# Moving the turn of a graph network's sums behind two chunks of the next pair, and the counts of edges behind the low parts

## The reference

```
layer 0:  a = (1 + eps) * x + segment_sum(x[src], dst)
          h = relu(batch_norm(a @ W1 + b1));  h = relu(batch_norm(h @ W2 + b2))   # W1 512x1024, W2 1024x512
          x1 = layernorm(x + (x + h))
layer 1:  a = segment_sum(x1[src], dst);  a = where(in_degree > 0, a, x1)
          h = relu(a @ W.T + b);  h = batch_norm(h)                                # W 512x512
          out = layernorm(x1 + h)
```

## Time and profile before

| | us |
|---|---|
| three runs | 2587.13, 2593.28, 2592.99; median 2592.99 |
| the profiled execution | 2588.04 |
| its span, first to last instruction | 2586.3 |
| busy: PE | 2295.0 (89%) |
| busy: POOL | 1602.0 (62%) |
| busy: DVE | 1364.4 (53%) |
| busy: ACT | 801.0 (31%) |

### The profile page before, as it was taken

How to read it: one execution, slowest core, us unless ns; L and a number is a source line. 1 busy time by engine, 2 the same in 40 slices (tenths; PEclk the granted TensorE clock), 3 DMA queues, 4 the chain that set the end, 5 groups by cost and what they waited for, 6 DMA issues and landing times. The chain is left out here.

```text
span 2586.3 us, 41697 instructions
## 1 busy us (share of the span) xinstructions
PE 2295.0 (89%) x9657; PEld 1505.0 (58%) x9658; DVE 1364.4 (53%) x2155; ACT 801.0 (31%) x1272; POOL 1602.0 (62%) x1729
## 2 busy tenths in 40 slices
PE   4999999999999999799995299999999999999964
PEld 2666666666666666688884255555555555555544
DVE  5555555555555555533336555455545555554557
ACT  1333333333333333455548411111111111111157
POOL 6777777777777777100002467777777777777712
PEclk9999999999999999899996699999999999999976
DMA  8777778787877877433216767777777777777758
GB/s 259 233 227 242 224 236 245 220 249 231 242 242 225 251 222 245 142 112 95 93 49 190 255 193 223 210 225 220 219 224 213 226 222 217 223 225 216 224 138 285
DMA packets 180571, 545.11 MB, mean 211 GB/s; under 512 B 48787, under 2 KB 51178, under 8 KB 175794
## 3 DMA queue, kind: packets, MB, share of 16 engines
q0 software_dynamic: 125120, 410.09, 53.5%
q1 hardware_dynamic: 33880, 78.23, 10.1%
q10 hardware_dynamic: 21544, 56.48, 6.5%
HBM read 493.06 MB, written 51.62 MB: 211 GB/s over the span
## 5 line engine op out<-in xcount | busy, mean ns | idle before, releaser
L780 PE MATMUL psum<-ring,select 128*125 x2600 | 1260.9, 608 | 11.0 <-issue 8.7
L555 POOL DMA_INDIRECT ring<-x_in,staged x782 | 799.1, 1022 | 246.2 <-issue 224.0
L555 POOL DMA_INDIRECT ring<-x_d,staged x782 | 748.2, 957 | 261.4 <-issue 226.4
L780 PEld LDWEIGHTS psum<-ring,select 128*125 128x125 f32 x2600 | 479.3, 191 | 380.3 <-issue 336.0
L651 DVE TENSOR_TENSOR rows_lo<-ring,rows_hi 128x512 fp32r<-128x512 f32 x500 | 329.8, 689 | 283.8 <-ACT rows_hi L867 283.2
L867 ACT ACTIVATE rows_hi<-ring 128x512 fp32r x500 | 295.0, 625 | 479.3 <-SPq L523 335.9
L808 PE MATMUL psum<-sumsT_hi,w_hi 128*128 128x250 f32 x1248 | 400.6, 321 | 4.3 <-DVE sumsT_lo L674 4.3
L765 PE MATMUL psum<-rows_hi,select_r 128*125 128x512 f32 x500 | 376.0, 752 | 7.5 <-DVE rows_lo L651 4.2
L808 PE MATMUL psum<-sumsT_lo,w_hi 128*128 128x250 f32 x1248 | 350.1, 281 | 0.0
L808 PE MATMUL psum<-sumsT_hi,w_lo 128*128 128x250 f32 x1248 | 348.4, 279 | 0.0
L808 PEld LDWEIGHTS psum<-sumsT_hi,w_hi 128*128 128x128 f32 x1248 | 237.3, 190 | 36.1 <-issue 32.6
(11 more groups left out here) (168 smaller groups left out, 2255.2 us busy)
## 6 DMA issues: line engine op xcount, KB each, us to landing
hidden_d<-of_layer ACTq DMA_DIRECT2D x25, 1000.0 KB, 5.4
act_f<-hidden_d SPq DMA_DIRECT2D x24, 1000.0 KB
ring<-x_in,staged POOLq DMA_INDIRECT x782, 3.8
ring<-x_d,staged POOLq DMA_INDIRECT x782, 3.7
own<-x_in ACTq DMA_DIRECT2D x50, 224.0 KB
own<-x_d ACTq DMA_DIRECT2D x50, 224.0 KB
ring<-x_d SPq DMA_DIRECT2D x10, 1120.0 KB
x_d<-done_r SPq DMA_DIRECT2D x9, 1120.0 KB
```

The lines of the kernel that those rows point to most:

```text
L555: nc.gpsimd.indirect_dma_start(slot(s), None, table, bass.IndirectOffsetOnAxis(ap=staged[:, s:s + 1], axis=0)).then_inc(gathered[s], 16)
L780: whole = nc.tensor.matmul(agg(h), select[h][:, WHOLE_AT.index(p), :], of_chunk(pe, first, place), start=False, stop=n + 1 == WINDOW, skip ...
```

## The change

The turn of the pair before is now called inside the first scatter of a pair, behind its first two chunks; only bank 0 is cleared ahead of them, and bank 1 inside `turn`, behind its wait for the sums. The address of that clear is taken from a register, which is 1 in a pair's first group and 2 later, so that it then hits a bank that the transposes write anyway. In layer 1 the two counting reductions are taken out of `selection` and called on their own: tile 0's behind `low_part`, tile 1's ahead of the next pair's selection.

```diff
--- before.py
+++ after.py
@@ -636,14 +636,14 @@
                     nc.vector.tensor_tensor(select[h][:, SPLIT:, :], m.column_ps[:, None, :].broadcast_to([P, rest, z.NT]),
                                             local[h][:, 2 * SPLIT:, None].broadcast_to([P, rest, z.NT]), ALU.is_equal
                                             ).then_inc(select_done[h], 1)
-                    if layer == 1:
-                        dve.wait_ge(select_done[h], 2 * v + 2)
-                        with nc.allow_low_precision(reason="counts up to WINDOW are exact in bfloat16"):
-                            nc.vector.tensor_reduce(edge_count[h][:, 0, :],
-                                                    select_r[h][:].bitcast(F32).rearrange("p k n -> p n k"),
-                                                    AX.X, ALU.add)
-                            nc.vector.tensor_reduce(edge_count[h][:, 1, :], select[h][:].rearrange("p k n -> p n k"),
-                                                    AX.X, ALU.add).then_inc(counted[h], 1)
+
+                def counts(v, h):
+                    dve.wait_ge(select_done[h], 2 * v + 2)
+                    with nc.allow_low_precision(reason="counts up to WINDOW are exact in bfloat16"):
+                        nc.vector.tensor_reduce(edge_count[h][:, 0, :],
+                                                select_r[h][:].bitcast(F32).rearrange("p k n -> p n k"), AX.X, ALU.add)
+                        nc.vector.tensor_reduce(edge_count[h][:, 1, :], select[h][:].rearrange("p k n -> p n k"),
+                                                AX.X, ALU.add).then_inc(counted[h], 1)
 
                 def low_rows(v, h, first, a, b):
                     for k in range(min(a, SPLIT), min(b, SPLIT)):
@@ -703,12 +703,16 @@
                         read_sums(v, tiles(pair, 1), 1)
                         low_rows(v, 0, first[0], 0, 2)
                         low_part(v)
+                        if layer == 1:
+                            counts(v, 0)
                         low_rows(v, 0, first[0], 2, 5)
                         selection(v, 1, tiles(i, 1), first[1])
                         low_rows(v, 0, first[0], 5, SPLIT)
 
                         read_sums(v, tiles(i, 0), 0)
                         low_rows(v, 1, first[1], 0, 4)
+                        if layer == 1:
+                            counts(v, 1)
                         next_pair = within(dve, (v + 1) // groups, z.PAIRS, "v counts below pairs times groups")
                         selection(v + 1, 0, tiles(next_pair, 0),
                                   first_chunk(dve, tiles(next_pair, 0), dve.snap((v + 1) % groups)))
@@ -746,12 +750,11 @@
                 def agg(h):
                     return m.bank(h)[0:z.NT, :]
 
-                def clear(i, h):
-                    pe.wait_ge(sums_done[h], i * groups + 1)
-                    nc.tensor.matmul(agg(h)[:, 0:1], m.zeros[:, 0:z.NT], m.ones[:, 0:1],
-                                     start=True, stop=False, skip_group_check=True)
-
-                def scatter(i, v, g, tile, h):
+                def clear(out):
+                    nc.tensor.matmul(out, m.zeros[:, 0:z.NT], m.ones[:, 0:1], start=True, stop=False,
+                                     skip_group_check=True)
+
+                def scatter(i, v, g, tile, h, between):
                     tile_use = pe.snap(2 * v + h)
                     first = first_chunk(pe, tile, g)
 
@@ -759,6 +762,8 @@
                     pe.wait_ge(sums_done[h], v + 1)
                     pe.wait_ge(select_done[h], 2 * v + 2)
                     for n, p in enumerate(ORDER):
+                        if n == 2:
+                            between()
                         if p in SPLIT_AT:
                             k = SPLIT_AT.index(p)
                             pe.wait_ge(split_lo, SPLIT * tile_use + k + 1)
@@ -784,10 +789,14 @@
                         if n + 1 in PRODUCT_AT[h]:
                             product(v, PRODUCT_AT[h][n + 1])
 
-                def turn(job):
+                def turn(job, bank=None):
+
                     pe.wait_ge(lo_done, 2 * job + 1)
                     for h in range(2):
                         pe.wait_ge(sums_done[h], job + 1)
+                    if bank is not None:
+                        at = within(pe, bank * m.BANK, 2 * m.BANK, "bank 1 or 2")
+                        clear(m.psum[0:z.NT, bass.ds(at, 1)])
                     for k in range(z.KD):
                         for h in range(2):
                             at = (k % (z.KD // 2)) * z.W + h * z.NT
@@ -819,14 +828,17 @@
                     pe.wait_ge(weights_lo, 1)
                     nc.tensor.matmul(count_ps[0:z.NT, 0:z.TILES], m.zeros[:, 0:z.NT], m.ones[:],
                                      start=True, stop=False, skip_group_check=True).then_inc(counts_zeroed, 1)
+                cleared = pe.alloc_register(f"pe_cleared{layer}")
                 with pe.Fori(0, z.PAIRS) as i:
-                    clear(i, 0)
-                    clear(i, 1)
+                    pe.wait_ge(sums_done[0], i * groups + 1)
+                    clear(agg(0)[:, 0:1])
+                    pe.reg_mov(cleared, 1)
                     with pe.Fori(0, groups) as g:
                         v = of_use(pe, i, groups, g)
-                        turn(v)
-                        scatter(i, v, g, tiles(i, 0), 0)
-                        scatter(i, v, g, tiles(i, 1), 1)
+
+                        scatter(i, v, g, tiles(i, 0), 0, lambda: turn(v, pe.snap(cleared, min_val=1, max_val=2)))
+                        scatter(i, v, g, tiles(i, 1), 1, lambda: None)
+                        pe.reg_mov(cleared, 2)
                 uses = pe.snap(groups * z.PAIRS)
                 turn(uses)
                 for b in range(HALVES):
@@ -1408,6 +1420,7 @@
 
         m.hidden_stored = nc.alloc_semaphore("hidden_stored")
         m.bank = lambda b: psum[:, b, :]
+        m.psum, m.BANK = psum[:].rearrange("p b c -> p (b c)"), 512
         m.banks = lambda a, b: psum[:, a:b, :]
         m.column_ps = psum[:, 6, 0:z.NT]
         m.column, m.ident = sb("column", [P, P]), sb("ident", [P, P])
```

## The result

Five runs of the kernel before and five of the changed one: median 2593.24 us before, 2580.76 us after (2572.14 to 2582.23); the ratio is 0.9945, 95% interval 0.9929 to 0.9962. That is 12.5 us less, where 2572 was predicted. The profiled execution of the changed kernel took 2581.07 us (span 2579.2), so beside the one before (2588.04) it shows only 7.0 us of the 12.5. The changed kernel's runs fall into two groups, 2572 to 2575 and 2581 to 2582, as those before did with 2587 and 2593; why, the traces don't say.

A forecast was written before the change was run, and what follows sets the result against it. PE and POOL were taken to run in step, with POOL's gathers limiting gains. Layer 1's 13.8 us and layer 0's 4.0 made 17.8, so 2570.2 from 2588.04; allowing for two run groups, 2572, range 2563 to 2581 (72%).

The forecast's parts named there:

- The bound: Both gather phases: PE and POOL run in step, and POOL's gather issue, 1.257 us each in layer 1, limits any gain.
- The rival in which PE gains all: Both layers: PE is the bound and its whole saving counts, about 64 us, giving 2524 us; chance 4%.
- The bubble: Each pair's end: PE's idle time between the clears of banks 0 and 1 goes, saving 1.2 us net, bounds 0.8 and 1.3.
- rival 2: Pair ends: the bubble comes back as another wait, only the start of layer 1 gains, 2583 us; chance 10%.
- POOL's gaps: Layer 1: the second gap, 1.26 us of excess, stays and five later ones, 4.7 us, vanish; layer 0's at 93.33 gives 1.0.
- Start of layer 1: First turn of layer 1: PE starts its chunks before the counts, so POOL's 7.92 us wait shrinks by 5.0, bounds 4.2 and 7.6.
- Tail of layer 1: End of layer 1: the last chunks' lead over PE shrinks from 4.3 to about 0.2 us, gaining 4.1, bounds 1 and 4.7.
- Layer 0: Layer 0: 1.0 us from the gap at 93.33 and 3 from a shorter stretch of slow gathers, 4.0 together.
- The step that failed: Layer 1's gathers: POOL's own length stays 0.957 us each; collisions with subtractions were priced in layer 0 only.
- The clock: Layer 1: PE, starved, falls to 1.2 GHz more often; at twice layer 0's share the time is 2624 us; chance 5%.
- The counts: Layer 1's moved reductions keep their cover of 8 us and cost 0; if cover were gone, up to 4.3 us a pair.
- The signs named ahead: Layer 1: POOL's waits on PE below 10 us, start gap about 3, last gather about 14 earlier, landing waits up, second clear unidled.

The follow-up runs named there:

- e0: The changed kernel itself, run again as reference and source of the second trace: median 2585.07 us, 0.9965 of the kernel before; its profiled execution took 2574.95 us.
- e4c: The changed kernel with only one of three terms of layer 1's product kept, leaving out low parts there: 2579.01 us, 0.9945 of the kernel before.
- e3b: The changed kernel with layer 1's subtraction reading its first operand from PSUM, so its low rows are wrong: 2567.23 us, 0.9898 of the kernel before.
- e5: The changed kernel with a second ACT copy of layer 0's split chunks into PSUM bank 7, which DVE subtracts from: 2580.55 us, 0.995 of the kernel before.
- e1: The changed kernel with the counts back in selection, so only the turn moved, on a slower chip: 3048.05 us against 3070.26 for the kernel before, 0.992.

## Why the prediction was right or wrong

**The number.** 17.8 us were added up and 12.5 measured (8.9 in the runs beside e0); 2580.76 us lies just inside the forecast's own range, whose upper end was 2581. By the profiled executions the sum is 17.8 and the measure 7.0, or 13.1 with the second trace. So the kind of gain was right and its size too large, and that the range held is in part luck: two terms for PE were off in opposite ways and cost nothing, and one was matched by chance.

**The bound: right.** POOL's gathers were named as what the time falls back to once PE runs freely. Layer 1's waits for landings and e4c show it. The rival in which PE gains all, 60 us, is out. The prediction called PE "only just the slower" in layer 1; by its own numbers, 39.27 us a pair against 31.28 gathers at 1.257 us, or 39.3, the two were even. That is why so little came of what PE saved.

**The bubble: right in kind, wrong in size, too small in layer 1 and too large in layer 0.** 1.2 us a pair were predicted, bounds 0.8 and 1.3. In layer 1 PE's pair took 36.67 us while it ran freely. Before, a pair at the full clock took 38.88 us (1565.10 to the next clear at 1603.98): 2.2 us are saved. From the clear of bank 0 to the first product it is 7.56 us for 9.74 one pair earlier; about half of that lies between the two clears and in the two chunks, and the rest is shorter pauses of PE behind them, such as the 0.41 us between the second clear and the transposes, now 0.03, which the sum didn't have. In the other seven of the 24 pairs before, the clock fell, and they took 40.6 us; so 39.27 was a mean of two kinds of pair. In layer 0 the bubble mostly came back as another wait. From 85 to 440 us PE's mean pair went from 39.25 to 38.91 us, 0.3 us less. PE's waits from 100 to 400 us, before and after:

```profile
PE psum L751 <- DVE sums L666: 9.4, 7, 1.5
...
PE psum L770 <- DVE rows_lo L651: 10.7, 14, 1.1
```

The first split chunk now stands right behind the transposes, and its low rows are not ready. That was rival 2, in one layer. Neither error cost the forecast much, since what PE saves in a pair is worth nothing where POOL is the bound.

**POOL's gaps.** In layer 1 the second stayed (1.25 us for 1.26) and the other five vanished (4.7 us), as said; so did the one at 93.33 us in layer 0 (1.0 us).

**Start of layer 1: right in kind, too large.** 5.0 us were predicted, 3.5 measured (7.62 to 4.10 of excess; 4.3 in the second trace). PE started its two chunks 8.1 us sooner on the clock, of which 2.0 are the earlier start of the layer, but they took 3.77 us for 2.91 before and the second clear comes behind them.

**Tail of layer 1: too large.** 4.1 us predicted, 2.6 measured. The prediction took the lead at the end of the last tile but one to shrink from 4.3 to 0.2 us. Its last chunk was issued at 2440.67 and taken at 2445.97: 1.6 us. PE had been stopped for landings earlier in that tile (1.56 us at 2433.36 and 0.79 at 2435.27), and the product behind them let the lead grow again.

**Layer 0: 4.0 predicted, 3.3 measured, but that they agree is chance.** The reason given for 3 of the 4 us, a shorter stretch of slow gathers, isn't seen: the mean gather is the same 1011 ns from 500 to 1000 us, and the time over 0.946 us a gather went from 59.8 to 57.9 us in all. The first gap, for which nothing was predicted, went from 4.14 to 2.88 us of excess, and it is 2.89, 4.14 and 5.40 in three other traces with the same layer 0 (e0, e3b, e4c); the gap at 55 us grew from 0.89 to 1.91. The spread of those four traces, 7.5 us at the last gather, is larger than the gain.

**The step that failed: the gathers of layer 1 keep their length.** The sum took 0.957 us as POOL's own in layer 1 and priced the collision of subtractions and gathers in layer 0 only. It grew in layer 1: the time over 0.946 us a gather went from 9.2 to 15.1 us (14.8, 17.6 and 17.2 in e0, e4c and e5), and with it 6.3 us of the 8.3 us that the waits gave back. e3b shows the cause, the subtraction with two SBUF inputs. Why the same number of meetings now costs more is open: that PE, ACT and DVE follow the landings, and so meet POOL's 1.25 us rhythm in a fixed phase, fits the rows but was only argued. The Trainium skill (SBUF — State Buffer, "SBUF: two separate sides") has the exclusion; the prediction named it and looked for it in the wrong layer. Of the 10.8 us between 17.8 and 7.0 this step is 6.3, start and tail 3.0 together, and the stretch between the layers 1.3, which is no more than traces of one code differ by (413.9 to 415.8 us in after, e0, e3b and e4c).

**The clock: the rival was wrong in sign.** PE, starved in layer 0, had 0.96; after the change it waits as much for landings and has 0.99. In the gather phases of the trace before, TensorE fell to 1.2 GHz 18 times (11 in layer 0, 7 in layer 1), each time right behind the idle piece before the clear of bank 1, 1.26 to 3.3 us long. After the change it fell three times, all in layer 0, each right behind an idle piece of 1.9 to 2.5 us at a pair's end; in the one at 763.67 PE, ACT and DVE all stand until 766 us, and no wait shows for PE. In the second trace it never fell, though it has four such pieces of 2.4 to 2.6 us. In layer 1 about twenty waits for landings of 1.3 us left the clock at 2.4 GHz. So neither the length of an idle piece alone nor a wait for landings decides; what does is open. The Trainium skill (TensorE: Matmul & The Clock Gate, "HAM oscillation — how this bites in real kernels") ties the falls to waits for transfers; here shorter waits of that kind, 1.8 us at the longest in layer 1, left the granted clock at 1.00.

**The counts: right.** DVE's selections kept their cover, PE waits for none of them, and gathers beside the reductions keep 0.95 us.

**The signs named ahead.** Met: ACT's waits for landings in layer 1, and the second clear without idle time. Missed: POOL's waits on PE in layer 1 fell from 22.6 to 13.0 us, not below 10; the gap at its start to 4.4, not 3 us; the last gather came 3.7 us earlier (8.0 in the second trace), not 14. None of the signs of being wrong appeared, the mean gather of layer 0 just so (1020 ns, limit 1022).

## What to carry to other kernels

Before a bubble of the busiest engine is priced by its count, compare that engine's period with the issue period of each engine that feeds it; here 39.27 against 39.3 us said that nearly all of PE's saving, 2.2 us a pair in layer 1, would turn into waiting for gathers. A wait that is taken away can come back one step further on, as the wait for the low rows did in layer 0. And before two traces are subtracted row by row, look at how far two traces of one kernel lie apart; here that was 7.5 us at the end of layer 0. When a pipeline becomes bound by issued gathers, look for what lengthens a gather: in both layers a VectorE operation with two SBUF inputs beside it did, and a PSUM operand took it away. Such a repair has to be priced by its latency too: a second copy on the way ended POOL's gathers 27 us sooner and gave that time to a wait for the low rows.

## What was not expected of the hardware

- Of 59 gathers of layer 1 that began inside a two-input subtraction (0.69 us, two in a row), 31 took 1.16 to 1.47 us instead of 0.95; in layer 0 such gathers took up to 1.99 us. Beside reductions of 3.97 us with one SBUF input every gather took 0.94 to 0.97 us. In all, the time over 0.946 us a gather was 56.5 us in layer 0 and 14.8 us in layer 1 (trace of e0).
- TensorE's granted clock rose with less busy time: 471 us busy of 500 at 0.96 before, 458 at 0.99 after. The falls to 1.2 GHz before stood right behind idle pieces as short as 1.26 us.
- The kernel before took 2587 to 2596 us on some chips and 3062 to 3155 us on others. The gathers themselves were no longer there (999 ns in layer 0 of e1, 1022 before at 2593); what differs is how long POOL waits for PE.
